# Graph attention: run ends put into PSUM in scan order, dot products added on TensorE, and the last layer's row products dealt out differently

## The reference, cut to what matters

```python
# layers one and two
xW = (x @ W).reshape(n, heads, out_ch)
alpha_s = jnp.sum(xW * a_src, axis=-1); alpha_d = jnp.sum(xW * a_dst, axis=-1)
e = leaky_relu(alpha_s[src] + alpha_d[dst], 0.2)
m = segment_max(e, dst); w = exp(e - m[dst]); z = segment_sum(w, dst)
out = segment_sum(xW[src] * (w / z[dst])[:, :, None], dst) + bias
# layer three: the score has a third term
h = (x @ W.T).reshape(n, H, D)
alpha = einsum('ehd,hd->eh', h[src], a_src) + einsum('ehd,hd->eh', h[dst], a_dst)
enc = relu(edge_attr @ edge_W.T + edge_b).reshape(-1, H, D)
alpha = alpha + jnp.sum(enc * h[dst], axis=-1)      # the dot products
alpha = leaky_relu(alpha, 0.2)                      # then softmax over each target, as above
```

## Time and profile before

| | |
|---|---|
| median of three runs | 2277.38 us |
| the profiled execution | 2274.25 us, its span 2272.3 us |
| busy: PE | 1671.5 us, 74% |
| busy: DVE | 1765.1 us, 78% |
| busy: ACT | 1051.6 us, 46% |
| busy: POOL | 1549.1 us, 68% |
| mean granted TensorE clock | 0.844 |
| batches of layer one | first adds at 115.4 us, last batch from 677.0 us |
| batches of layer two | 788.0 us to 1328.5 us |
| batches of layer three | 1452.5 us to 2229.7 us |

### The profile page before, as it was taken

One profiled execution on the slowest core, in us unless ns is written; L12 is line 12 of the kernel. 1 busy time (PEld: TensorE's weight loads), 2 busy tenths in 40 slices (PEclk: granted clock), 3 DMA queues, 4 the chain that ended last, 5 costly groups with the idle time before them and its releaser, 6 DMA issues.

```text
span 2272.3 us, 41838 instructions
## 1 busy us (share of the span) xinstructions
PE 1671.5 (74%) x8878; PEld 1022.6 (45%) x8878; DVE 1765.1 (78%) x5162; ACT 1051.6 (46%) x3550; POOL 1549.1 (68%) x1716
## 2 busy tenths in 40 slices
PE   5388877877875577777877766787778887777873
PEld 4245444444543344444544443454444444444441
DVE  5578888888889466666666677689898888989888
ACT  2234434444433344444445445445555555555554
POOL 3577777777747577777777747667666666666663
PEclk9577888888788688888788888789998899999985
DMA  5655544454431344444444511433343334344321
GB/s 165 154 157 141 141 139 136 140 140 139 140 120 60 106 134 134 137 134 137 134 134 134 179 58 63 117 97 112 112 118 113 104 110 111 111 117 117 111 66 57
DMA packets 129625, 274.31 MB, mean 121 GB/s; under 512 B 39681, under 2 KB 64380, under 8 KB 129363
## 3 DMA queue, kind: packets, MB, share of 16 engines
q0 software_dynamic: 64704, 182.91, 29.1%
q1 hardware_dynamic: 60257, 85.13, 12.4%
q10 hardware_dynamic: 4427, 3.60, 0.6%
HBM read 255.35 MB, written 17.20 MB: 120 GB/s over the span
## 4 chain that ended last, share of the span: by engine, by line
DVE 24%; PE 22%; POOL 19%; issue 18%; ACT 5%; DMA 5%; DVEq 3%; SPq 1%; ACTq 0%; POOLq 0%
POOL rows L1160 18%; PE bank L1546 13%; DVE sums L784 5%; DMA rows<-table,index_all 4%; ACT rows L1319 3%; PE bank L1565 2%; PE bank L1482 2%; DVE dots L800 2%; DVEq L810 2%; PE bank L1558 1%; DVE rows L773 1%; DVE runs L720 1%; DVE prod L793 1%; DVEq L784 1%; DVE seg L740 1%
## 5 line engine op out<-in xcount | busy, mean ns | idle before, releaser
L1160 POOL DMA_INDIRECT rows<-table,index_all x1320 | 1282.4, 972 | 549.9 <-issue 343.7
L1546 PE MATMUL bank<-rows,onehot 128*128 128x264 f32 (+1 forms) x2640 | 985.9, 483 | 222.5 <-ACT rows L1319 111.0
L784 DVE TENSOR_TENSOR sums<-sums,bank 128x264 f32 (+1 forms) x1320 | 550.3, 417 | 198.5 <-PE bank L1546 92.1
L1546 PEld LDWEIGHTS bank<-rows,onehot 128*128 128x128 f32 x2640 | 494.0, 223 | 441.4 <-issue 218.0
L1319 ACT ACTIVATE rows<-rows,wgt 128x33 f32<-128x33 f32 (+2 forms) x1840 | 511.2, 359 | 0.1
L1327 ACT ACTIVATE prod<-bank 128x512 f32<-128x512 f32 x240 | 134.0, 558 | 309.1 <-PE bank L1558 298.6
L1274 ACT CAST onehot<-bank 128x768 f32<-128x768 bf16 x240 | 177.3, 740 | 184.4 <-PE bank L1482 181.8
L773 DVE TENSOR_TENSOR rows<-rows,wgt 128x260 f32<-128x260 f32 (+2 forms) x480 | 199.8, 416 | 0.8 <-ACT wgt L1312 0.6
L1565 PE MATMUL bank<-late,onehotT 128*128 x1320 | 198.9, 287 | 0.3 <-DVE prod L793 0.3
L793 DVE TENSOR_TENSOR prod<-prod,bank 128x512 f32<-128x512 f32 x240 | 152.2, 634 | 30.7 <-PE bank L1565 24.0
L1482 PE MATMUL bank<-identb,onehotT 128*128 128x128 bf16 x1320 | 143.0, 257 | 28.5 <-DVE onehotT L647 23.3
(11 more groups left out here) (194 smaller groups left out, 1872.7 us busy)
## 6 DMA issues: line engine op xcount, KB each, us to landing
locb<-loc_d SPq DMA_DIRECT2D x120, 352.0 KB, 3.6
rows<-table,index_all POOLq DMA_INDIRECT x1320
flags<-flags_d SPq DMA_DIRECT2D x520, 27.5 KB
table<-rows SPq DMA_DIRECT2D x25, 136.0 KB, 1.8
table<-rows SPq DMA_DIRECT2D x25, 134.0 KB, 4.1
late<-table SPq DMA_DIRECT2D x1, 3300.0 KB, 15.7
table<-rows SPq DMA_DIRECT2D x25, 129.5 KB, 2.0
late<-table SPq DMA_DIRECT2D x1, 3212.5 KB, 17.1
```

The costliest lines, as they stand in the source:

```text
L784: done(v.tensor_tensor(a, a, sum_bank(l, t, s)[:, 0:VV], ALU.add), "add")
L1160: g.indirect_dma_start(out=rows[:, t.u, s, 0:ROW[l]], out_offset=None, in_=table[l], in_offset=bass.IndirectOffsetOnAxis(ap=index_all[:, t ...
L1546: done(m.matmul(sum_bank(l, t, s)[:, 0:VV], onehot[:, t.u, s, :], rows[:, t.u, s, 0:VV], start=True, stop=True), "agg")
```

## The change

**Links.** PE puts the ends into PSUM in the order in which DVE scans them: for each head first the carried maximum (a new matmul of a one by the last element of the former run, into column 0 of each group of B+1), then the B left ends, and separately the right ends in groups of B. The two scans read PSUM directly. The three copies into `ends` and the instruction for the new maximum are gone. DVE subtracts the carried value from the found one; ACT takes the ReLU of that and then exp(-x). The chain penalties are laid out flat, and their two DMAs for each batch write to the new places.

**Dot products.** In layer three `dots` is laid out by head and slot, and PE adds it to the scores while it turns them: two matmuls into the same PSUM tile in place of a transposition. The leaky ReLU of layer three comes after it, on the transposed scores in `tops`.

**Owners.** In layer three DVE multiplies slots 0, 1, 3 (before 1, 4, 7), ACT 2, 5, 8 (before 0, 2, 10), and POOL 4, 6, 7, 9, 10 (before 3, 5, 6, 8, 9).

```diff
@@ -61,7 +61,7 @@
...
-OWNER = ("VAVVAVAVVVV", "VAAAAAAAAAA", "AVAPVPPVPPA")
+OWNER = ("VAVVAVAVVVV", "VAAAAAAAAAA", "VVAVPAPPAPP")
@@ -139,7 +139,7 @@
...
-        chain = sb("chain", [1, RING, 2, 8, B + 1])
+        chain = sb("chain", [1, RING, 8 * (2 * B + 1)])
@@ -152,15 +152,14 @@
...
-        ends = sb("ends", [1, 2, 8 * (B + 1)])
...
-        newtop = sb("newtop", [1, 8])
+        rise = sb("rise", [1, 8])
...
-        dots = sb("dots", [P, RING, B, 8])
+        dots = sb("dots", [P, RING, 8, B])
@@ -241,7 +240,7 @@
...
-        ps_row = ps_T[0:1, 256:256 + 2 * 8 * B]
+        ps_left, ps_right = ps_T[0:1, 256:256 + 8 * (B + 1)], ps_T[0:1, 352:352 + 8 * B]
@@ -351,6 +350,14 @@
...
+        def links_left(t, H):
+            return chain[0:1, t.u, 0:H * (B + 1)]
+        def links_right(t, H):
+            return chain[0:1, t.u, 8 * (B + 1):8 * (B + 1) + H * B]
         def batches(eng, body):
@@ -658,19 +665,14 @@
...
-                    if SELF[l]:
-                        done(v.tensor_copy(score[:, 1, 0:H * B].rearrange("p (h s) -> p s h", h=H), ad[:, :, H:n]),
-                             "sc2")
-                        done(v.tensor_tensor(sc, rows[:, t.u, :, VV:VV + H], ad[:, :, 0:H], ALU.add), "sc3")
-                    else:
+                    if not SELF[l]:
...
-                        need(dve, "dot", (t.k + 1) * G)
-                        need(dve, "sc2", kk + 1)
-                        done(v.tensor_tensor(sc, sc, dots[:, t.u, :, :], ALU.add), "sc3")
+                        return
+                    done(v.tensor_copy(score[:, 1, 0:H * B].rearrange("p (h s) -> p s h", h=H), ad[:, :, H:n]), "sc2")
+                    done(v.tensor_tensor(sc, rows[:, t.u, :, VV:VV + H], ad[:, :, 0:H], ALU.add), "sc3")
...
-                    if SELF[l]:
-                        need(dve, "sc2", kk + 1)
+                    need(dve, "sc2", kk + 1)
...
                 def tops(t, l=l, H=H):
@@ -680,6 +682,9 @@
...
+                    if not SELF[l]:
+                        done(v.scalar_tensor_tensor(s0, s0, SLOPE, s0, ALU.mult, ALU.max), "sc")
+                        need(dve, "sc", kk + 1)
@@ -698,36 +703,20 @@
                 def links(t, l=l, H=H):
...
-                    R = H * (B + 1)
-                    e = [ends[0:1, i, 0:R].rearrange("p (h s) -> p h s", h=H) for i in range(2)]
-                    r = [ps_row[:, i * 8 * B:i * 8 * B + H * B].rearrange("p (h s) -> p h s", h=H) for i in range(2)]
-                    run = runs[0:1, 0, 0:R].rearrange("p (h s) -> p h s", h=H)
+                    R, R1 = H * B, H * (B + 1)
...
+                    need(dve, "link", kk)
...
-                    done(v.tensor_copy(e[0][:, :, 1:], r[0]), "ends0")
-                    done(v.tensor_copy(e[1][:, :, 0:B], r[1]), "ends1")
-                    need(dve, "runl", kk)
-                    done(v.tensor_copy(e[0][:, :, 0:1], run[:, :, B:B + 1]), "ends2")
-                def links2(t, l=l, H=H):
-                    kk = l * K + t.k
-                    R = H * (B + 1)
-                    need(dve, "ends2", kk + 1)
-                    need(dve, "ends0", kk + 1)
-                    need(dve, "ends1", kk + 1)
-                    need(dve, "link", kk)
-                    pen = [chain[0:1, t.u, i, 0:H, :].rearrange("p h s -> p (h s)") for i in range(2)]
-                    done(v.tensor_tensor_scan(runs[0:1, 0, 0:R], pen[0], ends[0:1, 0, 0:R], -BIG,
+                    done(v.tensor_tensor_scan(runs[0:1, 0, 0:R1], links_left(t, H), ps_left[:, 0:R1], -BIG,
...
-                    done(v.tensor_tensor_scan(runs[0:1, 1, 0:R][:, ::-1], pen[1][:, ::-1], ends[0:1, 1, 0:R][:, ::-1],
-                                              -BIG, ALU.add, ALU.max), "runr")
+                    done(v.tensor_tensor_scan(runs[0:1, 1, 0:R][:, ::-1], links_right(t, H)[:, ::-1],
+                                              ps_right[:, 0:R][:, ::-1], -BIG, ALU.add, ALU.max), "runr")
+                    need(dve, "runl", kk + 1)
...
-                    c = ends[0:1, 0, 0:R].rearrange("p (h s) -> p h s", h=H)[:, :, 0]
-                    b = runs[0:1, 1, 0:R].rearrange("p (h s) -> p h s", h=H)[:, :, 0]
-                    done(v.tensor_tensor(newtop[0:1, 0:H], c, b, ALU.max), "rnew")
-                    need(dve, "rnew", kk + 1)
-                    need(dve, "rscale", kk)
-                    done(v.tensor_tensor(drop[0:1, 0:H], c, newtop[0:1, 0:H], ALU.subtract), "rdrop")
+                    need(dve, "rrise", kk)
+                    carried = runs[0:1, 0, 0:R1].rearrange("p (h s) -> p h s", h=H)[:, :, 0]
+                    found = runs[0:1, 1, 0:R].rearrange("p (h s) -> p h s", h=H)[:, :, 0]
+                    done(v.tensor_tensor(drop[0:1, 0:H], found, carried, ALU.subtract), "rdrop")
...
                 def finish_tops(t, l=l, H=H):
@@ -797,8 +786,10 @@
...
-                    done(v.tensor_reduce(dots[:, t.u, lo:hi, :].rearrange("p s h -> p (s h)"),
-                                         prod[:, i % 2, 0:(hi - lo) * D].rearrange("p (g c) -> p g c", c=CH[2]),
+                    if i == 0:
+                        need(dve, "scT", l * K + t.k - 2)
+                    done(v.tensor_reduce(dots[:, t.u, :, lo:hi].rearrange("p h s -> p s h"),
+                                         prod[:, i % 2, 0:(hi - lo) * D].rearrange("p (s h c) -> p s h c", h=8, c=CH[2]),
...
                 def bias_add(b, l=l):
@@ -986,10 +972,11 @@
...
-                    for i, at in ((0, 1), (1, 0)):
-                        row = chain_d[i:i + 1, bass.ds(t.k * B, B)]
-                        sp.dma_start(chain[0:1, t.u, i, 0:H, at:at + B],
-                                     row.unsqueeze(1).to_broadcast([1, H, B])).then_inc(s_meta[l][t.u], 16)
+                    for i, to in enumerate((links_left(t, H).rearrange("p (h s) -> p h s", h=H)[:, :, 1:],
+                                            links_right(t, H).rearrange("p (h s) -> p h s", h=H)[:, :, 0:B - 1])):
+                        n = B - i
+                        sp.dma_start(to, chain_d[i:i + 1, bass.ds(t.k * B, n)].unsqueeze(1).to_broadcast([1, H, n])
+                                     ).then_inc(s_meta[l][t.u], 16)
...
                 def write(b, u, l=l):
@@ -1286,16 +1273,19 @@
...
-                    for i in range(2):
-                        r = a.copy(linkrow[0:1, i, 0:H * B].rearrange("p (h s) -> p h s", h=H),
-                                   runs[0:1, i, 0:H * (B + 1)].rearrange("p (h s) -> p h s", h=H)[:, :, i:i + B])
-                    done(r, "link")
+                    to = [linkrow[0:1, i, 0:H * B].rearrange("p (h s) -> p h s", h=H) for i in range(2)]
+                    a.copy(to[0], runs[0:1, 0, 0:H * (B + 1)].rearrange("p (h s) -> p h s", h=H)[:, :, 0:B])
+                    done(a.copy(to[1][:, :, 0:B - 1], runs[0:1, 1, 0:H * B].rearrange("p (h s) -> p h s", h=H)[:, :, 1:]),
+                         "link")
...
                 def rescale(t, l=l, H=H):
...
+                    need(act, "rscale", kk)
+                    done(a.activation(rise[0:1, 0:H], drop[0:1, 0:H], ACT.Relu), "rrise")
+                    need(act, "rrise", kk + 1)
...
-                    done(a.activation(scale[0:1, 0:H], drop[0:1, 0:H], ACT.Exp), "rscale")
+                    done(a.activation(scale[0:1, 0:H], rise[0:1, 0:H], ACT.Exp, scale=-1.0), "rscale")
...
                 def expw(t, l=l, H=H):
@@ -1499,6 +1489,14 @@
...
                 def scoresT(t, l=l, H=H):
...
+                    if not SELF[l]:
+                        need(pe, "diff", kk)
+                        need(pe, "dot", (t.k + 1) * G)
+                        m.matmul(ps_T[0:H * B, 0:P], dots[:, t.u, :, :].rearrange("p h s -> p (h s)"), ident[:, :],
+                                 start=True, stop=False)
+                        need(pe, "sc2", kk + 1)
+                        done(m.matmul(ps_T[0:H * B, 0:P], score[:, 0, 0:H * B], ident[:, :], start=False, stop=True), "scT")
+                        return
@@ -1506,10 +1504,15 @@
...
                 def endsT(t, l=l, H=H):
...
-                    need_apart(pe, ("top", kk + 1))
-                    for i, e in enumerate((P - 1, 0)):
-                        r = m.transpose(ps_row[:, i * 8 * B:i * 8 * B + H * B], top[0:H * B, 2, e:e + 1],
-                                        ident[0:H * B, 0:H * B])
+                    need(pe, "runr", kk)
+                    need(pe, "fresh", l + 1)
+                    need(pe, "top", kk + 1)
+                    left = ps_left[:, 0:H * (B + 1)].rearrange("p (h s) -> p h s", h=H)
+                    m.matmul(left[:, :, 0], ones[0:1, :], runs[0:1, 0, 0:H * (B + 1)].rearrange(
+                        "p (h s) -> p h s", h=H)[:, :, B], start=True, stop=True)
+                    m.transpose(left[:, :, 1:], top[0:H * B, 2, P - 1:P],
+                                ident[0:H * B, 0:H * B])
+                    r = m.transpose(ps_right[:, 0:H * B], top[0:H * B, 2, 0:1], ident[0:H * B, 0:H * B])
```

(23 more changed lines are left out.)

## The result

The changed kernel takes 2184.51 us (median of 4 runs, 2179.91 to 2195.31) against 2278.09 for the kernel before: a ratio of 0.9591, 95% interval 0.9569 to 0.9612, 94 us less. The forecast was 2201, its range 2165 to 2245. A second comparison gave 0.9545 (0.9522 to 0.9568). The profiled execution shown here took 2195.31 us, the slowest of its kernel, 79 us under the profiled one of before.

A forecast was written before the change was run, and what follows sets the result against it. DVE plus a 0.81 us loop bounds layer three, POOL's gathers layers one and two. Savings of 58 + 5 + 8 + 2 + 3 = 76 us from 2274.25 give 2198; the runs' median lies 3.1 higher: 2201, range 2165 to 2245.

The forecast's parts named there:

- Links, gain 1.45: DVE's links block in layer three falls from 2.35 to 0.9 us a batch; bound 0.55 if scans stay at 0.74.
- Scores, gain 0.4: DVE's scores block in layer three, 1.04 us: one instruction stays (0.31), ReLU moves (0.30); gain 0.4 us, bounds 0 to 0.7.
- Owners, DVE's 0.81: Layer three: PE's 1.33 us wait for ACT before slot 0 goes, and DVE's 0.47 + 0.34 with it; bounds 0.4 to 0.81.
- the 1.0 us of new waits: Layer three, each batch: ACT's late slots 5 and 8 make engines coupled by two sum banks wait, giving 17.8 us.
- the 16.86: DVE's time for a layer three batch in us, 19.52 - 1.45 - 0.4 - 0.81, if it never waits more than before.
- the 14 us for slower batches: Layer three's cost of batches with a lower clock, 21.02 against 19.52 us; forecast to fall to 9, saving 5.
- 8 us from the layer's other batches: Layer three's first two and last four batches, outside the 34, save 1.4 us each.
- PE at 15.8 busy: PE's work in a layer three batch: 15.29 us before plus 0.5 for the added matmuls.
- B: Rival, 0.17: POOL keeps the port or ACT keeps PE waiting; scans stay at 0.74; 32 us less, 2245.
- C: Rival, 0.07: DVE's saved time turns into waiting, PE's idle time being unavoidable; about 5 us saved, 2272.
- A: Rival, 0.15: POOL back to back, DVE without new waits, no clock dips; layer three 16.9 a batch; 116 less, 2161.
- D: Rival, 0.05: slower; ACT's 1.8 us blocks for slots 5 and 8 fully exposed on PE; 37 us more, 2314.

The follow-up runs named there:

- the last experiment: Changed kernel with the subtraction's carried maximum read from PSUM and layer three's run ends turned one step later: 2161.61 us, 0.9480 of the kernel before.

## Why the prediction was right

**The bound.** DVE in layer three, POOL in layers one and two: right, by the two layers that gained nothing and by the 84.6 us in the third.

**Links, gain 1.45.** The mechanism was right, the size was too high for the change as it is. The scans shrank to 0.33 and 0.30, but I gave the subtraction 0.1 us, though it keeps two SBUF inputs and stands in POOL's multiplies. It took 0.61 on average. The block is 1.47 or 0.98 us, 1.23 on average, a gain of 0.9 to 1.4. With the subtraction from PSUM it is 0.93.

**Scores, gain 0.4.** 1.04 - 0.27 - 0.31 = 0.46. Right. PE's two matmuls (0.38 and 0.45 us for the one of 0.31) cost 0.5 more by their rows, 0.35 foretold with a bound of 0.7, and the wait of 1.06 in front of them is gone.

**Owners, DVE's 0.81.** The wait of 0.47 went, of the other 0.31 is left: 0.50. The forecast took the whole 0.81.

**The term that was mis-sized** is the 1.0 us of new waits. PE does wait 0.81 us for ACT before slot 8 (0.9 foretold), but almost nothing of it reaches DVE, which idles 0.01 us before slot 3's add, where 0.5 was foretold, and 0.02 before slot 8's. What DVE still waits for PE, 0.36 us before slot 1's add, is the rest of an old wait, and the 0.70 before slot 4's is the register load, which the 16.86 already held. That PE's lead of up to two slots swallows the wait is likely, but no run shows it. So the undisturbed batch is 17.53 or 17.05 and not 17.8. For the 34 batches that is an estimate, from the rows, of 34 us too many foretold for new waits, against 12 us for the old wait that stayed and 11 for the stretched links block; and of the 14 us for slower batches nearly all went (clock 0.99), not 5. Together they leave some 20 us, which is the step from the foretold 63 to 84.6.

**Outside the 34 batches** I foretold 8 us from the layer's other batches. In the profile shown they cost 2 us more than before, because of the first one; in that of the second comparison they save 7. So the two profiles give 79 and 101 us in all for the 76 foretold, of which the 34 batches give 84.6 and 89.6.

**PE at 15.8 busy.** It was 14.9 to 15.1. Eleven small matmuls for the target scores (line 1495 before, 1485 after) took 35.0 us in 34 batches and take 20.5, the same 0.18 us each but packed closer. With only two of the three parts they took 31.6 or more, and with the ends a step later 37.7. I have not found out why.

**The signs.** The scans at 0.33 during POOL's multiplies, DVE at 92% and PE at 87%, POOL's waits for PE at 39.5 us and slot 8 in slot 0's place all came. The links block under 1 us did not, in most batches.

**The rivals.** B's scans at 0.74 did not occur. C's idle PE was not unavoidable here, but on the slower chip the result is C's: no gain, with DVE at 74%, though PE wasn't full either (77%). A's floor of 16.9 a batch was reached only by the last experiment, after one more cause on DVE and one on PE were taken out. D did not occur.

**The part the forecast did not see** is why owners and links are worth 71 us together and 48 apart. I added the gains of the parts as if all of DVE's saved time came out. With the links alone half of it came back as waits, since the loop over slot 0 set the pace (idle time 78.0 to 103.1 us); the owners break that loop, and only then does the links' gain come out. Collisions with POOL don't explain the surplus: they cost about the same with and without the links, 11.6 and 9.6 us.

## What to carry to other kernels

When the bound engine's instructions are stretched by another engine's, price its small instructions by where they fall in the other's timeline, not by their length: a copy of eight numbers cost 0.15 or 1.42 us. Moving one operand to PSUM took the stretch away at no cost to DVE, though the gain in time was small here (about 5 us), and after such an edit the remaining two-SBUF instruction is the next to look at. Test two edits together as well as apart: an edit to the busiest engine gives back its gain as waits while a loop through other engines sets the pace, and the busy and idle times of that engine show it even where the total time comes out as expected. And before you add a wait to a forecast, ask whether the engines' room to run ahead of each other swallows it; before you believe a wait's label, look whether the named engine was done before the gap began.

## What the runs showed of the hardware

VectorE instructions wait for GpSimd's multiply if they read two SBUF tensors or copy SBUF to SBUF: 0.89 against 0.15 us for the subtraction, 3.56 against 0.41 for the backward scan, 0.61 on average against 0.15 for the carry copy. None with an input in PSUM was stretched in any batch of layer three: in the changed kernel's 34 batches the sums' add stayed at 0.41 to 0.43 us in all 65 cases beside a multiply, the new scans at 0.33 and 0.30 in all 34. Nor was the reduction over channels (one SBUF input, 0.68 us). But the comparison that makes the one-hot matrix (one bf16 tensor and a scalar from SBUF) took 0.83 in place of 0.57 us in the one batch of layer three of the kernel before where it met a multiply. With one input in PSUM the subtraction took 0.152 to 0.156 us in every batch.

The Trainium skill ("GPSIMD Engine Reference", 1 Specifications) states the contention for two SBUF inputs and 2-port modes, and these rows agree. That a single DVE instruction can be held for five GpSimd instructions in a row, as the scan was, these rows add; so does the GpSimd multiply that took 0.92 us in place of 0.63 beside a DVE multiply.

A PSUM source costs the scans nothing: 0.33 us against 0.34 in the earlier trace rows. The Trainium skill ("VectorE: DVE Perf Modes", the errata-adjusted cycle table) has 62 cycles more for a PSUM source, and these rows do not agree.

And one chip ran the kernel before 16% slower and the changed kernel 21% slower, with stops of 2 to 6 us on several engines, and there the gain of 4% was not to be had.
